# Attention on TensorE: the second bank of transposes issued between the two pairs of value matmuls

## The reference, cut to what matters

```python
scores = jnp.einsum('bhqd,bhkd->bhqk', q, k) / SMAX
mask = jnp.triu(jnp.full((Sq, Sq), -999.0, dtype=scores.dtype), k=Sq - 1)
p = jax.nn.softmax(scores + mask, axis=-1)
att = jnp.einsum('bhqk,bhkd->bhqd', p, v).transpose(0, 2, 1, 3).reshape(Bq, Sq, AHD)
```

## Time and profile before

| what | value |
|---|---|
| median of 3 runs | 2468.53 us (2466.96 to 2470.21) |
| the profiled execution, its own time | 2464.61 us |
| its span, first to last instruction | 2462.8 us |
| mean granted TensorE clock | 0.994 |
| PE busy | 2404.3 us (98%) |
| VectorE busy | 1866.7 us (76%) |
| ScalarE busy | 1680.8 us (68%) |
| GpSimd busy | 1529.1 us (62%) |

### The profile page before, as it was taken

One profiled execution on the slowest core, in us unless ns is written; L12 is line 12 of the kernel. 1 busy time (PEld: TensorE's weight loads), 2 busy tenths in 40 slices (PEclk: granted clock), 3 DMA queues, 4 the chain that ended last, 5 costly groups with the idle time before them and its releaser, 6 DMA issues.

```text
span 2462.8 us, 46531 instructions
## 1 busy us (share of the span) xinstructions
PE 2404.3 (98%) x14504; PEld 2086.9 (85%) x14504; DVE 1866.7 (76%) x3594; ACT 1680.8 (68%) x2913; POOL 1529.1 (62%) x1550
## 2 busy tenths in 40 slices
PE   7999799999999999999999999999999999999999
PEld 6988688888888888888888888888888889988888
DVE  6777777878878787887878878787887865556665
ACT  4554477878778787887878778787787864443333
POOL 2333477777777777777777777777777755542220
PEclk9999999999999999999999999999999999999999
DMA  4522531213222122221213212122221345331111
GB/s 175 199 102 94 171 116 47 87 57 97 72 65 94 43 85 77 85 94 43 85 60 94 84 53 94 43 85 83 79 94 43 108 167 172 119 128 35 48 51 43
DMA packets 127894, 220.15 MB, mean 89 GB/s; under 512 B 6778, under 2 KB 89620, under 8 KB 118932
## 3 DMA queue, kind: packets, MB, share of 16 engines
q1 hardware_dynamic: 127764, 218.78, 27.5%
HBM read 114.95 MB, written 53.48 MB: 68 GB/s over the span
## 4 chain that ended last, share of the span: by engine, by line
PE 81%; DVE 8%; issue 6%; POOL 2%; ACT 2%; DMA 0%; DVEq 0%; SPq 0%; ACTq 0%; POOLq 0%
PE a_ov L1574 19%; PE a_sc L1538 18%; PE a_tr L1550 18%; PE a_pj L1493 7%; PE a_pj L1502 4%; PE g_acc L879 3%; PE g_hid L840 3%; PE f_acc L879 2%; PE f_hid L840 2%; PE m_proj L1976 2%; PE m_hid L2042 1%; DVE f_hp L679 1%; POOL m_zin L1828 1%; PE m_acc L2013 1%; PE f_aux L817 1%
## 5 line engine op out<-in xcount | busy, mean ns | idle before, releaser
L1453 DVE TENSOR_REDUCE a_nmax<-a_sc 128x1 f32<-128x1024 f32 x512 | 626.8, 1224 | 262.4 <-PE a_sc L1538 254.0
L1378 POOL TENSOR_SCALAR a_pr<-a_pr,a_rden 128x1024 f32<-128x1024 f32 x512 | 576.2, 1126 | 258.8 <-DVE a_rden L1458 189.6
L1299 ACT ACTIVATE a_pT<-a_tr 128x512 fp32r<-128x512 f32 x1024 | 559.9, 596 | 209.1 <-PE a_tr L1550 207.6
L1464 DVE TENSOR_TENSOR a_pT<-a_tr,a_pT 128x512 fp32r<-128x512 f32 x1024 | 650.1, 677 | 15.6 <-ACT a_pT L1299 15.6
L1574 PE MATMUL a_ov<-a_pT,a_v_s 128*128 128x512 f32 x2048 | 600.2, 415 | 3.1 <-DVE a_half L1444 2.0
L1305 ACT ACTIVATE a_pr<-a_sc,a_nmax 128x1024 f32<-128x1024 f32 x512 | 573.4, 1120 | 32.5 <-DVE a_nmax L1453 28.9
L1538 PE MATMUL a_sc<-a_k_s,a_q_s 128*128 128x512 f32 x2048 | 555.2, 393 | 6.7 <-DMA a_k_s<-a_k_s 6.7
L1550 PEld LDWEIGHTS a_tr<-f_ident,a_pr 128*128 128x128 f32 x4096 | 473.9, 140 | 89.5 <-DVE a_pT L1464 17.8
L1550 PE MATMUL a_tr<-f_ident,a_pr 128*128 128x128 f32 x4096 | 537.6, 273 | 6.9 <-DVE a_pT L1464 6.9
L1538 PEld LDWEIGHTS a_sc<-a_k_s,a_q_s 128*128 128x128 f32 x2048 | 380.5, 188 | 87.3 <-DMA a_k_s<-a_k_s 6.9
L1574 PEld LDWEIGHTS a_ov<-a_pT,a_v_s 128*128 128x128 f32 x2048 | 347.5, 189 | 54.2 <-issue 4.9
(11 more groups left out here) (214 smaller groups left out, 3273.8 us busy)
## 6 DMA issues: line engine op xcount, KB each, us to landing
a_z_s<-zT SPq DMA_DIRECT2D x32, 1024.0 KB, 7.9
a_k_s<-a_k_s SPq DMA_DIRECT2D x64, 512.0 KB, 5.9
a_wqk_s<-w_split SPq DMA_DIRECT2D x64, 256.0 KB, 3.2
a_v_s<-a_v_b SPq DMA_DIRECT2D x16, 1024.0 KB, 4.6
att<-a_ao SPq DMA_DIRECT2D x32, 512.0 KB, 2.9
m_in<-att SPq DMA_DIRECT2D x16, 1024.0 KB, 6.0
a_wv_s<-w_split SPq DMA_DIRECT2D x17, 512.0 KB, 3.8
zT<-f_zT SPq DMA_DIRECT2D x8, 1024.0 KB, 3.9
```

The lines of the kernel that those rows point to most:

```text
L1299: act.activation(pT[:, (u // 4) % 2, 0, 4 * part:4 * part + 4, (u % 4) * P:(u % 4 + 1) * P], tr[:, part].rearrange("p (t q) -> p t q", t=4 ...
L1378: pool.tensor_scalar(pr[:, k % NP], pr[:, k % NP], rden[:, k % NP:k % NP + 1], 1.0, ALU.mult, ALU.mult).then_inc(s["normed"], 1)
L1453: dve.tensor_reduce(nmax[:, k % NP:k % NP + 1], sc[:, k % 2], AX.X, ALU.max, negate=True).then_inc(s["negmax"], 1)
L1464: dve.tensor_tensor(to[:, 1], tr[:, part].rearrange("p (t q) -> p t q", t=4), to[:, 0].bitcast(F32), ALU.subtract).then_inc(s["tr_lo"], 1)
```

## The change

The second bank's four transposes, with their wait for `tr_lo` and their count on `tr`, move behind the first pair of value matmuls of the step (`kt == 2 * q`), where the step has value matmuls. Where it has none, they stay directly behind the first bank's. The waits at the head of a block (`q == 0`) stay where they are, ahead of the first value matmul. Nothing is added or taken away, and the programs of the other engines are not touched.

```diff
+                def transposes_of(part):
+                    if part == 0:
+                        pe.wait_ge(s["normed"], u - LAG + 1)
+                    if not (first and k == LAG):
+
+                        pe.wait_ge(s["tr_lo"], 2 * (u - LAG) + part - 1)
+                    for j in range(4):
+                        o = pe.transpose(tr[:, part, j * P:(j + 1) * P],
+                                         pr[:, (k - LAG) % NP, (4 * part + j) * P:(4 * part + j + 1) * P], ident[:])
+                    o.then_inc(s["tr"], 1)
+
                 if transposes_at(k, first, last):
...
+                    transposes_of(0)
                 v = values_at(k, first)
+                if not (v and not (last and v[2] >= 0)) and transposes_at(k, first, last):
+                    transposes_of(1)
                 if v and not (last and v[2] >= 0):
...
                             o = pe.matmul(ov[:], v_s[:, vslot, kt, 2 * vhead:2 * vhead + 2]
                                           .rearrange("p k f -> p (k f)"), pT[:, blk % 2, a, kt],
                                           start=(kt == 0 and a == 0), stop=(kt == QT - 1 and a == 1))
+                        if kt == 2 * q and transposes_at(k, first, last):
+                            transposes_of(1)
```

More of the change, by code:

```diff
@@ L1542, in body @@
                     o.then_inc(s["sc"], 1)
-                if transposes_at(k, first, last):
[L1544 to L1552, removed]
+                def transposes_of(part):
[7 more added lines that the diff above has]
+                    o.then_inc(s["tr"], 1)
+                if transposes_at(k, first, last):
+                    transposes_of(0)
                 v = values_at(k, first)
+                if not (v and not (last and v[2] >= 0)) and transposes_at(k, first, last):
+                    transposes_of(1)
                 if v and not (last and v[2] >= 0):
```

## The result

| what | before | changed |
|---|---|---|
| median | 2469.37 us (4 runs, 2466.96 to 2470.58) | 2568.56 us (4 runs, 2565.06 to 2573.21) |
| the profiled execution, its span | 2462.8 us | 2571.4 us |
| ratio | | 1.0407 (1.0394 to 1.0420) |

The change makes the kernel 99 us slower, 4.1%. The forecast was 2560 us, in a range of 2528 to 2590.

A forecast was written before the change was run, and what follows sets the result against it. PE was taken to bound the attention, with its nearest wait at each block's head. Block waits of 96.1 us, plus 2 for changes of kind, less 4 regained, made 94 us: 2558.7, stated as 2560 us, range 2528 to 2590.

The forecast's parts named there:

- PE is the bound in the attention, and the block's reads are the nearest wait: Attention: PE busy 1657.78 of 1669.00 us; a block's first value waits for ACT's and DVE's reads, now 0.04 us.
- Part one: Ordinary steps: second bank ready 0.46 us later, ACT's exponentials 0.41, DVE's second low part 0.17, covered away from blocks.
- The cover: Ordinary steps: margins of 0.12 us on ACT and 0.06 on DVE were to absorb the later second bank.
- Part two: Block steps: PE arrives earlier, ACT's read ends 0.41 us later; waits 0.76 (first head) and 0.90 (second), 96.1 us in all.
- An iteration's first block: 16 blocks that also wait for split values: new wait 0.90 to 0.92 us, 0.65 lost each, 10.4 us in all.
- my upper bound: An iteration's first block: 0.85 us lost instead of 0.65 if the 0.23 of "issue" comes on top.
- The gain at the transposes: PE's waits for DVE at the transposes, 6.9 us, mostly behind blocks: 4 us taken as gained.
- The term for the changes of kind: PE changing between transposes and values twice a step: 0 to 5 us over 512 steps, taken as 2.
- The first rival: Blocks: ACT's read not put off, only the earlier arrival costs; 47 us, 2512 us in total; chance 0.09.
- The estimate from the Trainium skill's page: Blocks: with 81 ns per 128-column and 131 ns per 512-column matmul, about 0.48 us lost each, total near 2526 us.
- Two of my marks: New profile: PE's attention busy time hardly grows; block waits put down to ACT's read of `ov` total about 105 us.
- the other rivals: Transpose waits vanish, 2460 us (0.02); no measurable change (0.02); waits in other steps, 2618 (0.06); clock halved, near 2994 (0.01).

The follow-up runs named there:

- e3: Kernel before, with the second bank between the value pairs only in a block's two middle steps (q = 1 and 2): 2464.49 us, ratio 0.9991.
- e1: Kernel before, with the second bank's transposes between the value pairs in block steps (q = 0) alone: 2517.34 us, ratio 1.0209.
- e2: Kernel before, with the second bank between the value pairs in all steps but the block steps: 2509.90 us, ratio 1.0181.
- e4: Kernel before, with the second bank between the value pairs only in a block's last step (q = 3): 2510.38 us, ratio 1.0176.
- e5: Changed kernel, with ACT reading 256 of 512 columns in 90 of 128 blocks: 2551.25 us, ratio 1.0350 to the kernel before.
- e9: Kernel before, with the projection ahead of the values in block steps that have one: 2448.90 us, ratio 0.9936.
- e7: e6 with the projection ahead of the values in block steps that have one: 2451.46 us, ratio 0.9939 to the kernel before.
- e6: Kernel before, with the second bank between the value pairs only in the step behind a block step (q = 1): 2465.36 us, ratio 0.9996.
- e10: Kernel before, with the projection ahead of the values in every step that has both: 2453.46 us, ratio 0.9949.
- e11: e3 with the projection ahead of the values in block steps that have one: 2449.98 us, ratio 0.9946 to the kernel before.

## Why the prediction was right

- **PE is the bound in the attention, and the block's reads are the nearest wait**: right. The waits at the blocks are 88.0 us more in 14 of 16 iterations (97.0 less 9.0); for 16 that would be 100.6, against 98.7 that the attention is longer.
- **Part one, the second bank 0.46 us late, ACT's exponentials 0.41**: right; 2.03 instead of 1.61 us after the first transpose is 0.42. DVE's pair of low parts takes 1.45 instead of 1.27, the 0.17 forecast. The cover held in ordinary steps: e3 loses nothing.
- **Part two, 0.76 and 0.90 us of wait at a block**: right, 0.77 and 0.91 measured. The sum of two causes is shown by e1 (50 us) and e2 or e4 (43 us), and the reader that ends it by e5.
- **An iteration's first block** was the term that I sized too small: I took 0.90 us, and it waited 1.11. The 0.23 of "issue" came on top, as my upper bound had it; 0.84 lost instead of 0.65, 16 times, is 3 us. PE starts there 0.25 us behind the end of ACT's read and not 0.05, before the change and in e1, e2 and e4 too. What the 0.20 are stays open.
- **The gain at the transposes**, 4 us, came out at about 3 by the steps behind blocks (2.9 in 14 iterations). The row that I had taken it from did not shrink (7.6 us, 6.9 before); the one of the weight loads at the same place did, from 17.8 to 11.3. The term for the changes of kind, 2 us, is too small to be told: the steps that neither begin a block nor follow such a step are 0.7 us longer over 14 iterations (224 steps), which would be 1.6 for 512.
- So the terms give 64 x 0.73 + 48 x 0.85 + 16 x 0.84 - 3 = 98 us. Of the 8.6 us between my 2560 and the median, these are 4; 3.5 are the two longer runs, and 1 is left.
- **The first rival** (half of the loss) was priced at 47 us; e1 is that case by construction and has 50. There its 0.33 for the first head was 0.44 (0.48 less 0.04): the release by DVE takes 0.15 us and not 0.05. The place of the release did not matter to the forecast, since ACT is last there.
- **The estimate from the Trainium skill's page** ("TensorE: Matmul & The Clock Gate", "Back-to-back issue gap") came to 2526 us with the page's spacings. The changed kernel lies 39 us above that at the least, and its spacings are those of the trace before: four transposes from start to start plus the gap took 0.35 (1263.03 to 1263.38) and the pair of values 0.55 (to 1263.93).
- **Two of my marks were wrong**: I expected PE's busy time in the attention hardly to grow, and it grew by 20.5 us (1657.78 to 1678.27). The wait put down to ACT's read was to be about 105 us, and the profile names 79.0. Both have one reason: PE's records hide a part of the waits, as the two last rows of the first timeline show (0.52 against 0.76).
- **A reading was loose**: I wrote that the clock fell after an idle time of 6.68 us. By the earlier trace rows it fell at 305.48, within that time, which ran from 301.99 to 308.67.
- Ordinary steps did not grow. In the changed kernel's profile the granted clock stayed at 1.00 without a break from 330.92 to 2109.27 us, through all the new waits (both profiles have a stretch of 3.4 us at 0.50 in the last 5 us of the attention). So the other rivals fall.

## What to carry to other kernels

When PE is packed, an order on PE that only permutes work can still cost, since every instruction that stands between a result and its next writer is cover for the engines that read it. Before moving work past a wait, write down the wait's slack (here 0.04 us) and how the readers' release moves; an in-order reader passes on any lateness of the input ahead of it. The same arithmetic finds gains: work of PE's that nobody needs soon belongs ahead of such a wait, and here that gave 0.6% with nothing added.

## What the runs showed of the hardware

- The end of a reader is not the start of the waiting matmul, and the gap depends on the reader. Behind ACT's read PE starts 0.05 us after the recorded end, behind DVE's copy 0.15 us (the smallest values in the kernel before, the changed one and e1 alike). At an iteration's first block it is 0.25 behind ACT's.
- A jump back of the loop on ACT holds its sequencer for 2.34 to 2.54 us in the kernel before (2.36 to 2.62 in e9, 2.35 to 2.64 in the changed one), and the loop's exit does not. On the other engines the same gap is 0.06 to 0.26 us (before: PE 0.06, SP 0.13 to 0.15, POOL and DVE 0.22 to 0.26).
- ACT's read of the second head's rows starts 1.23 us behind the exponentials' start, that of the first head's 1.09 (medians; 1.22 and 1.09 in the changed kernel), for the same length of the exponentials. The cause was not tried.
- During a wait of PE for a DMA of some 6.7 us at the start of the attention, the granted clock fell to half in both profiles. Before, it was half for 6.83 us; in the changed kernel's profiled run for 27.30 us, for the same program:

```profile
303.62:330.92 27.30, 22.81 (x91) 21.16 (x92) 11.59 (x29) 9.57 (x17) 12.57 (x21) 0.50 0.25 68
345.00:2113.00 1768.00, 1678.27 (x9596) 1390.15 (x9597) 1399.38 (x2221) 1360.05 (x2337) 1259.74 (x1285) 1.00 0.23 72
```

  The columns are those of rows 4. The first value matmul came at 345.3 us instead of 337.2, about the 7 us by which this run and another lie above the other two. The program up to there is the same, so I do not put it down to the change, and the length of this stretch differs between profiles of the other kernels too. It is 6.83 us in e1 and e3 and 13.65 in e2, e4 and e7, with the first value matmul at 336.8 to 337.9 and at 338.7 to 339.8 us. Runs with a mean clock of 0.991 or 0.992 occur in e5, e6, e7, e10, e11 and in the kernel before as well. What sets the length is open.
